# Masked attention stages: where the output matmuls stand in steps with two fills of the small bank

## The reference

```
q, k, v = norm(x) @ wq, keys @ wk, keys @ wv         # keys: ctx, or norm(x) in stages 2 and 3
a = softmax(where(mask, -inf, q @ k.T / sqrt(16)))   # masks in stages 0 and 2, causal in stage 3
x = x + (a @ v) @ wo + bo
x = x + gelu(norm(x) @ w1 + b1) @ w2 + b2            # stages 0, 2 and 4
```

## Time and profile before

| | us |
|---|---|
| median of 3 runs | 5176.82 |
| lowest, highest | 5170.62, 5177.7 |
| time of the profiled execution | 5179.82 |
| its span, first to last instruction | 5177.0 |
| TensorE (PE) busy | 4691.9 (91%) |
| DVE busy | 3024.5 (58%) |
| ScalarE busy | 2308.0 (45%) |
| GpSimd busy | 963.8 (19%) |
| mean granted TensorE clock | 0.969 of full speed |

### The profile page before, as it was taken

The page is one execution under the profiler, slowest core; times in us unless marked ns, Lnnn a source line. Parts: engine busy times, 40 slices in busy tenths (PEclk is TensorE's granted clock), DMA queues, the critical chain, the costliest instruction groups (busy, mean ns, idle before and its releaser), DMA issues.

```text
span 5177.0 us, 71932 instructions
## 1 busy us (share of the span) xinstructions
PE 4691.9 (91%) x24484; PEld 1889.5 (36%) x24484; DVE 3024.5 (58%) x7970; ACT 2308.0 (45%) x3011; POOL 963.8 (19%) x831
## 2 busy tenths in 40 slices
PE   6899999989998999999888988998867999999999
PEld 2333333333332333343444433333333333333333
DVE  6777676556677766666456674555512554554554
ACT  4455554466664444444445444444432333333332
POOL 0111111010110111111111101101111333333333
PEclk9999999999999999999999999999988999999999
DMA  1111111121111100011111211111111000000000
GB/s 58 35 59 41 46 40 43 34 89 53 65 60 44 41 32 32 30 34 47 63 60 59 70 57 47 36 34 38 40 35 53 1 13 13 13 13 13 1 13 9
DMA packets 152347, 202.10 MB, mean 39 GB/s; under 512 B 18994, under 2 KB 102322, under 8 KB 150707
## 3 DMA queue, kind: packets, MB, share of 16 engines
q1 hardware_dynamic: 151986, 197.31, 11.5%
HBM read 128.86 MB, written 68.42 MB: 38 GB/s over the span
## 4 chain that ended last, share of the span: by engine, by line
PE 58%; issue 20%; DVE 11%; ACT 4%; DMA 4%; POOL 1%; SPq 1%; DVEq 1%; ACTq 0%; POOLq 0%
PE psO L701 7%; PE small L630 7%; PE small L637 6%; PE psT L676 6%; PE psT L903 4%; PE psS L658 4%; PE psT L759 3%; DVE nmb L1139 2%; PE psT L630 2%; PE psT L868 2%; PE psO L918 2%; PE psT L637 2%; PE psT L918 2%; ACT probs L961 2%; DMA oN<-o_mid 2%
## 5 line engine op out<-in xcount | busy, mean ns | idle before, releaser
L961 ACT ACTIVATE probs<-psT 128x1024 f32<-128x1024 f32 (+3 forms) x1280 | 1159.8, 960 | 1009.2 <-PE psT L676 824.3
L1139 DVE TENSOR_REDUCE nmb<-psS 128x1 bf16<-128x512 f32 x1024 | 649.0, 684 | 288.6 <-PE psS L658 287.7
L1136 DVE CUSTOM_DVE_ANT_0 out<-psS,pens_sb 128x512 f32<-128x512 f32 x1024 | 665.5, 685 | 254.4 <-issue 253.1
L676 PE MATMUL psT<-low 32*128 32x512 f32 (+3 forms) x5120 | 757.4, 611 | 46.5 <-ACT probs L961 29.2
L658 PE MATMUL psS<-out 32*128 32x512 bf16 (+3 forms) x2560 | 594.0, 378 | 109.7 <-DVE nmb L1136 50.5
L701 PE MATMUL psO<-probs,V 128*32 128x512 f32 (+3 forms) x5120 | 668.0, 595 | 1.2 <-ACT probs L961 1.0
L1337 DVE TENSOR_REDUCE parts<-psS 128x2 bf16<-128x1024 f32 x256 | 314.9, 1230 | 522.1 <-PE psS L890 522.1
L1076 ACT ACTIVATE probs<-psT 128x1024 f32<-128x1024 f32 x256 | 262.0, 1023 | 526.1 <-PE psT L906 526.1
L658 PEld LDWEIGHTS psS<-out 32*128 32x128 bf16 x2560 | 147.4, 91 | 844.2 <-issue 488.9
L759 PE MATMUL psT<-out,W 128*128 128x512 f32 x768 | 378.9, 619 | 0.5
L1454 POOL TENSOR_TENSOR oN<-oN,probs 128x1024 f32<-128x1024 f32 x128 | 300.6, 2348 | 316.2 <-ACT probs L1076 315.8
(11 more groups left out here) (163 smaller groups left out, 5877.8 us busy)
## 6 DMA issues: line engine op xcount, KB each, us to landing
o_mid<-out SPq DMA_DIRECT2D x160, 256.0 KB, 2.0
oN<-o_mid SPq DMA_DIRECT2D x160, 128.0 KB
oN<-r_mid SPq DMA_DIRECT2D x80, 256.0 KB
x_mid<-xe SPq DMA_DIRECT2D x40, 512.0 KB, 2.9
xw<-x_mid SPq DMA_DIRECT2D x36, 512.0 KB, 4.0
xe<-x_mid SPq DMA_DIRECT2D x36, 512.0 KB, 4.9
cT<-ctxT SPq DMA_DIRECT2D x20, 512.0 KB, 7.4
W<-wm SPq DMA_DIRECT2D x6, 1024.0 KB, 8.0
```

Source lines behind the costliest of these rows:

```text
L676: last = nc.tensor.matmul(psT[j][:, q0:S], Kf[rows_of(j), q, a, c, kt * P:(kt + 1) * P], Qf[rows_of(j), q, a, c, q0:S], start=True, stop=p ...
L961: nc.scalar.activation(probs[:, i % 2, two, q0:S], psT_all[:, two, q0:S], ACT.Exp, scale=float(DH) ** -0.5)\
L1136: nc.vector.tensor_tensor_reduce(junk[:, e, 0:n], psS[e][:, 0:n], penalty, 1.0, -3.0e38, ALU.add, ALU.max, at).then_inc(sem[f"s_read{e}"], 1)
L1139: nc.vector.tensor_reduce(at, psS[e][:, 0:n], AX, ALU.max).then_inc(sem[f"s_read{e}"], 1)
```

## The change

One condition is added in TensorE's loop. `limited` chooses whether the outputs stand behind the late fill. It is now false in masked stages too in the steps that have both an early and a late fill; there the outputs stand between the fills, as in the other stages. In masked steps with a late fill alone nothing changes. Where a step has maxima beside the fills and its late fill is a whole `q` or `k` projection, the outputs come ahead of those maxima; no masked step with two fills is of that kind.

```diff
                     of = prev if i == 0 else None if after_mlp else cur
-                    limited = of is not None and of.s in MASKED
+                    limited = of is not None and of.s in MASKED and not (place.body.at(2 * i) and late)
                     if of is not None and not limited:
                         outputs(place, of, (i - 1) % STEPS)
```

## The result

The changed kernel takes 5152.44 us (median of 8 runs, 5137.81 to 5166.07) against 5177.66 for the kernel before in the same session (8 runs, 5170.62 to 5180.77). The ratio is 0.9949 with a 95% interval of 0.9937 to 0.9961.

What follows compares the result with a forecast made beforehand. The order of work on TensorE, busy 91% of the span, was taken to set the time. Terms -12.2 - 5.1 + 2.9 + 0.3 - 2.5 + 4 = -12.6 us gave 5167.2 for the profiled execution, 5164.2 as median, range 5155 to 5173.

Steps and rivals of the forecast that it cites:

- Step 9: Masked units with an MLP, outputs between fills `h0` and `h1`: 0.87 us gained 14 times, 12.2 us.
- Step 6: Stage 0 units with an MLP, outputs between fills `y23` and `c0`: 0.85 us gained 6 times, 5.1 us.
- Steps 0 and 3: Fills `m1`, `v2` and `x0`, `x1` in 14 masked MLP units: TensorE's gain given back at `x0`, 2.9 us lost.
- `y01`: Output projection after `x0`, `x1`: waits for scaling or ScalarE; +0.15 us in eleven units, +0.40 in three.
- two further steps 0: Fills `m1`, `v2` in units whose current stage is 1 or 3: 0.15 us lost each, 0.3 us.
- The clock: Longer idle around `x0`, `x1` brings more falls of TensorE's clock to half: 4 us lost, bounds 0 and 9.
- Rivals 1 and 4: Half clock after `x0`, `x1`: gain given back, 5171 us, chance 0.18; or low past `y01`, 5192 us, chance 0.05.
- The opening units: 11 masked steps in the two units without an MLP opening stages 0 and 2: 2.5 us gained, bounds 0 and 4.4.
- Rival 3: All waits before the late fills go, as DVE's chain has slack or absorbs the 0.15: -31 us, 5146, chance 0.07.
- Rival 2: At `h0`, `h1`, exponentials or the take of `h1` gate the MLP: 0.3 us instead of 0.87, time 5172, chance 0.14.
- Rival 5: Change doesn't do what it says: outputs wait for DVE's limit where it was seen as done; no effect, chance 0.01.

## Why the forecast was half right

**Step 9: right.** Forecast 0.87 in 14 units, 12.2 us; 0.86 and 12.0 in the trace, 12.4 alone on the chip. The exponentials don't gate the block; what was sized on the unmasked unit of the earlier trace rows held.

**Step 6: right.** 0.85 six times. It wasn't run alone; the 5.1 us are the trace's.

**Steps 0 and 3 up to the next scores: right.** `v2` 0.14 to 0.15 later, 1.8 of waiting before `x0` (of which the trace books 0.55 one step earlier), outputs waiting 0.81 and 1.13 for the limit (forecast 0.8 and 1.1), next scores 0.3 earlier relative to `x0` in stage 0 and 0.3 later in stage 2. `x0` comes 11.47 after `v2` in the units above, before and after, and so 0.14 later in the unit, as forecast. DVE paces this stretch, as the runs with early statistics show: with 0.75 us taken from DVE's chain `x0` moves by 0.65.

**`y01`: the step that failed.** The forecast has `y01` wait for GpSimd's scaling, "behind DVE's reciprocal, two DMA hops and so 0.15 later". It takes the hops as fixed, in line with its premise that "the schedule repeats from unit to unit to a hundredth of a microsecond"; the second hop never did, with 1.6 to 4.1 us over the inner units of the kernel before. It follows the chain through its last releaser and leaves out what else the moved instruction starts: in step 0 the outputs of the unit before reach ScalarE, SyncE's store and the gather 1.8 us earlier. Their transfers are off the path by their own landing, but the hop gets shorter when they are issued earlier. The hop alone became 11.1 us shorter over the 12 inner units. Their time from start to `y01` went from 311.9 to 309.8, 2.1 us less (311.7 in the second profile), which holds the longer clock stretches (below) and the 0.14 of each step 0 against it. In the last units of stages 0 and 2, where the weights stand behind the gather, and in the two units after them it went down by 1.92, 2.14, 1.77 and 2.32, together 8.2 us. The forecast had a loss of 2.9, one of 0.3 for two further steps 0 and 4 of clock for the same stretches, +7.2 in all; the trace has -10.3 (-8.7 in the second profile), and the runs with steps 0 and 3 alone sum to -8.8. This is more than the whole error.

The two units behind the masked stages (current stage 1 or 3) were forecast at a loss of 0.15 each. DVE has no limit to run behind the take of `v2` there. In the kernel before it stood idle instead, 0.89 us in the first of them, for the next scores; these now come earlier, the idle is gone, and `x0` comes 0.84 and 0.93 us earlier. The pace of the masked units was carried over to units whose pacing is another.

**The clock: near in size, but put down to the wrong step, and not seen in the sum.** The falls between `x0` and `y01` rose from 7 units to 10, and to 8 in the second profile; 12 of 14 have one in the kernel with the held store. Yet step 3 isn't what brings them. Without early statistics, the four profiles that leave step 0 as it was have 7, 5, 3 and 6 falls (the kernel before; step 9, step 3 and the opening units alone), the five that change it 10 and 8 (the changed kernel), 8 (step 0 alone), 8 (without step 3) and 12 (store held). So the falls go with step 0, behind which the wait before `x0` is longer; the outputs' wait in step 3, which the forecast counts with it, is there in the run with 3 falls and absent from two of those with 8. That the longer wait causes them wasn't tried by itself. Among the inner units after the change, the stretches of stage 0 take 10.85 to 11.00 with a fall and at most 10.45 without, those of stage 2 mostly 11.58 with and 10.00 without. Stage 0 has one fall more than before and stage 2 two: 0.55 + 2 x 1.58 = 3.7 us, where the forecast has 4. This is worked out from the two profiles, and partly luck: it goes with the count, which is 8 in one further profile of the same kernel. The shorter hop takes off more in the same stretches, and elsewhere falls became fewer: the mean clock of the program is 0.969 in both. The rule of the Trainium skill, "TensorE: Matmul & The Clock Gate", section "A second HAM failure mode: psum-queue depth-cycling", says that short idles between groups of matmuls make the clock swing and cost throughput. Single stretches agree (more units at half clock behind a longer wait, 0.5 to 1.6 us each); taken as a forecast for the kernel it doesn't hold: not all 14 units fall, and half-clock time doesn't rise in sum. Rivals 1 and 4 fall with it.

**The opening units: not to be told.** 2.5 us forecast, nothing measured alone, with 6 us of interval to either side [0.9989, 1.0012]. In the profile of the changed kernel one is 3.1 us longer, with half-clock time up from 2.5 to 9.7, and one 4.1 shorter, with it down from 22.2 to 11.2. The order isn't needed for that: with steps 9 or 3 alone, which leave the opening units as they were, the second one is 3.3 us shorter too (97.5 against 100.7).

**The sum.** By the runs -12.4 (step 9), -9.8 (step 0), +1 (step 3) and 0 (opening), with -5.1 of the trace for step 6: -26.3, and 0.9949 of 5177.66 is -26.4. Each of the runs' terms is uncertain by about 5 us. Rival 3's size, -31, is near, but not its mechanism: not all waits went, the one before `x0` grew. (Its 11 us for steps 0 and 3 count 0.8 once a unit; 0.8 in each of the 30 steps would be 24.) Rival 2 didn't come: step 9 gave its 12 us. Rival 5 holds for the two first steps 0 only, as it says itself.

What stays open: whether the kernel is really 8 to 10 us better without step 3, why the clock falls in some units and not in others, and how the gather lengthens the hop. That its transfers still occupy the DMA engines then is argued from the intervals below, not shown.

## What to carry to other kernels

Follow a moved instruction through every queue that its result goes on to, stores and gathers too, and not only through the releaser that the trace shows as the last: it can speed up or slow down transfers of others that seem to have their own chain. When a wait moves from one place to the next, find the engine that paces the stretch between them and put its work into its idle time; a move of 0.75 us of DVE's work was worth as much here as all of TensorE's reordering, though most of it came in stages that the reordering doesn't touch. And read the wait at the next meeting point too: where `y01` still waited for the hop, an earlier `x0` gave nothing.

## What the runs showed of the hardware

The time of the small transfer that carries the reciprocals (L507 to the issue of L512, which waits for it) goes by how long before it the gather (L502) was issued. In the inner units of the masked stages, over the kernel before, the changed kernel in both its profiles, steps 9, 0 and 3 alone and the change without step 3:

| gather issued before the hop | units | the hop takes |
|---|---|---|
| 8.05 us and more | 48 | 1.46 to 1.48 us |
| 5.9 to 6.6 us | 29 | 1.46 to 2.96 us |
| 4.1 to 4.7 us | 7 | 3.6 to 4.1 us |

The three kernels that leave step 0 as it was have all of the lower two rows. The 48 units of the first row are those of the four with step 0 changed. With early statistics on top of the change the distance is 7.0 to 8.3 us in 24 units, and the hop takes 1.46 to 1.74. In the unmasked stage 1 of the profiles in the table, the unit that fetches new weights aside, 7.5 us still go with 2.3 to 2.8 and 8.6 us with 1.5 to 2.5, so the distance isn't all of it.

The runs of one kernel spread with the granted clock: those of the changed kernel range from a span of 5134.9 us at a mean of 0.974 to 5163.7 at 0.965. That is 29 us, more than the whole change is worth.
